# Second cross-attention of a two-layer decoder: the side work of each slot in another order

## The reference, cut to what matters

```
q, k, v = per head: x_h @ Wq.T, c_h @ Wk.T, c_h @ Wv.T
energy  = einsum('nqhd,nkhd->nhqk', q, k)
att     = softmax(energy / 16)
out     = einsum('nhql,nlhd->nqhd', att, v) @ Wo.T + bo
x       = layernorm(x + out)
```

## Time and profile before

| what | value |
|---|---|
| median of 3 runs | 2770.71 us (2766.24 to 2780.35) |
| the profiled execution | 2786.15 us |
| its span, first to last instruction | 2784.3 us |
| mean granted TensorE clock | 0.939 |
| PE busy | 2576.5 us (93%) |
| DVE busy | 1465.8 us (53%) |
| ACT busy | 1129.4 us (41%) |
| POOL busy | 1075.1 us (39%) |
| maxima of this stage on DVE (L1253) | 512 of 683 ns, 323.9 us busy |
| exponentials of this stage on ACT (L1203) | 256 of 1025 ns, 257.3 us busy |

### The profile page before, as it was taken

The page is one execution under the profiler, slowest core; times in us unless marked ns, Lnnn a source line. Parts: engine busy times, 40 slices in busy tenths (PEclk is TensorE's granted clock), DMA queues, the critical chain, the costliest instruction groups (busy, mean ns, idle before and its releaser), DMA issues.

```text
span 2784.3 us, 36664 instructions
## 1 busy us (share of the span) xinstructions
PE 2576.5 (93%) x13730; PEld 1534.9 (55%) x13734; DVE 1465.8 (53%) x3205; ACT 1129.4 (41%) x1614; POOL 1075.1 (39%) x727
## 2 busy tenths in 40 slices
PE   5786999999999999998799999958899999989997
PEld 3343555556556655664466666636344343468886
DVE  3444555555555555553533333347678777454545
ACT  3544344444444444443122222223377778731111
POOL 4666366765766666565000000052323333110001
PEclk8997899999999999999799999979699899889998
DMA  2001100000000000000899999720001000000000
GB/s 105 9 9 34 37 12 12 27 25 13 27 12 20 18 12 12 20 7 16 316 385 385 385 385 388 299 59 4 26 19 29 18 19 13 14 20 23 19 22 33
DMA packets 61345, 228.94 MB, mean 82 GB/s; under 512 B 17624, under 2 KB 31600, under 8 KB 45296
## 3 DMA queue, kind: packets, MB, share of 16 engines
q1 hardware_dynamic: 55280, 209.28, 20.5%
q0 software_dynamic: 3584, 9.84, 1.2%
q10 hardware_dynamic: 2304, 7.49, 0.7%
HBM read 214.37 MB, written 9.70 MB: 80 GB/s over the span
## 4 chain that ended last, share of the span: by engine, by line
PE 81%; DVE 7%; issue 4%; ACT 3%; POOL 3%; DMA 3%; SPq 0%; POOLq 0%; ACTq 0%; DVEq 0%
PE PS L686 8%; PE PS L1499 7%; PE PS L2098 7%; PE PS L669 6%; PE PS L717 5%; PE PS L1116 5%; PE PS L1131 5%; PE PS L1517 4%; PE PS L727 4%; PE PS L2086 4%; PE PS L701 3%; PE PS L1149 3%; PE PS L750 2%; DMA m_fb<-in_m_fb 2%; PE PS L673 2%
## 5 line engine op out<-in xcount | busy, mean ns | idle before, releaser
L950 POOL TENSOR_TENSOR x_A<-x_A,x_P 128x1024 f32<-128x1024 f32 x190 | 451.2, 2375 | 205.8 <-ACT x_P L797 191.8
L877 DVE CUSTOM_DVE_ANT_0 x_junk<-PS,x_mb 128x512 bf16<-128x512 f32 x512 | 330.9, 684 | 354.7 <-PE PS L701 354.4
L1253 DVE TENSOR_REDUCE y_Mx<-PS 128x1 f32<-128x512 f32 x512 | 323.9, 683 | 103.1 <-PE PS L1149 101.3
L797 ACT ACTIVATE x_P<-PS,x_kb 128x1024 f32<-128x1024 f32 x256 | 271.9, 1112 | 226.6 <-PE PS L673 224.6
L1203 ACT ACTIVATE y_P<-PS 128x1024 f32<-128x1024 f32 x256 | 257.3, 1025 | 99.4 <-PE PS L1131 96.8
L1499 PE MATMUL PS<-m_w,m_xt 128*128 128x512 f32 x624 | 282.9, 597 | 0.6 <-issue 0.6
L686 PE MATMUL PS<-x_P,x_V 128*64 128x512 f32 x1024 | 246.4, 602 | 0.0
L669 PE MATMUL PS<-x_Q,x_K 64*128 64x512 f32 x1536 | 231.6, 405 | 0.0
L2098 PE MATMUL PS<-n_xp,n_wp 128*128 128x512 f32 x816 | 212.0, 409 | 4.3 <-POOL n_wp L2214 4.3
L1149 PE MATMUL PS<-y_K,y_Q 16*128 16x512 f32 x512 | 192.1, 530 | 2.9 <-ACT y_F L1213 1.4
L1131 PE MATMUL PS<-y_Q,y_K 32*128 32x512 f32 (+1 forms) x1024 | 193.1, 461 | 0.3 <-ACT y_P L1203 0.2
(11 more groups left out here) (332 smaller groups left out, 4219.5 us busy)
## 6 DMA issues: line engine op xcount, KB each, us to landing
m_w<-in_m_w SPq DMA_DIRECT2D x39, 2048.0 KB, 11.3
m_fb<-in_m_fb SPq DMA_DIRECT2D x39, 1024.0 KB, 13.3
m_v<-in_m_w SPq DMA_DIRECT2D x39, 1024.0 KB, 7.1
x_w<-in_x_w SPq DMA_DIRECT2D x32, 384.0 KB, 3.1
ys<-m_yb SPq DMA_DIRECT2D x39, 128.0 KB
n_wg<-in_n_w SPq DMA_DIRECT2D x17, 256.0 KB, 2.8
x_cT<-in_ctxT SPq DMA_DIRECT2D x4, 1024.0 KB, 6.1
y_c<-in_ctxT SPq DMA_DIRECT2D x6, 512.0 KB, 3.7
```

The lines of the kernel that those rows point to most:

```text
L797: act.e.activation(Pt[gt % 6][:], PS[:, 2 * i:2 * i + 2, :], ACT.Exp, bias=kb[u // 8 % 2][:, kt:kt + 1], scale=scale).then_inc(s["exp"], 1)
L877: dve.e.tensor_tensor_reduce(junk[j % 2][:], ring.bank("max", v, j), mb[b % 2][:, half * 512:half * 512 + 512], 1.0, -3e38, ALU.add, ALU.m ...
L950: pool.e.tensor_tensor(A[u % 2][:], Pt[(gt - 1) % 6][:] if kt == 1 else A[u % 2][:], Pt[gt % 6][:], ALU.add).then_inc(s["add"], 1)
L1253: dve.e.tensor_reduce(Mx[v % 2][:, h, qt, half:half + 1], ring.bank("max", v, j), AX.X, ALU.max).then_inc(s["red"], 1)
```

## The change

Only the two tables of `l1_cross` change. In `beside`, k 1 goes from slot 1 to slot 2, q from 2 to 4, v 0 and 1 (with even units only) from 3 and 4 to 1 and 3, wo and res 0 to 3 from 3, 4, 5, 6 to 1, 3, 5, 7, and turn from 5 to 6. The transposes tp 0 and 1 leave `behind` of slots 4 and 6 for `beside` of slots 5 and 7. In `behind`, st 0 to 3 go from slots 4, 5, 6, 7 to slots 2, 4, 6 and slot 0 of the unit after, and nr 0 to 3 from slots 1 to 4 to slots 2 to 5. mq stays in slot 5, rec in 3, mul in 5, ev in 0.

```diff
-            beside = {0: [("k", 2, 0)], 1: [("k", 2, 1)], 2: [("q", 2, 0)], 3: [("v", 2, 0), ("wo", -2, 0), ("res", -2, 0)],
-                      4: [("v", 2, 1), ("wo", -2, 1), ("res", -2, 1)], 5: [("turn", 1, 0), ("wo", -2, 2), ("res", -2, 2)],
-                      6: [("wo", -2, 3), ("res", -2, 3)], 7: []}
-            behind = {0: [("ev", -1, 0), ("xb", 0, 0)], 1: [("nr", -3, 0)], 2: [("nr", -3, 1)], 3: [("rec", -1, 0), ("nr", -3, 2)],
-                      4: [("st", -2, 0), ("nr", -3, 3), ("tp", -3, 0)], 5: [("mul", -1, 0), ("st", -2, 1)],
-                      6: [("st", -2, 2), ("tp", -3, 1)], 7: [("st", -2, 3)]}
+            beside = {0: [("k", 2, 0)], 1: [("v", 2, 0), ("wo", -2, 0), ("res", -2, 0)], 2: [("k", 2, 1)],
+                      3: [("v", 2, 1), ("wo", -2, 1), ("res", -2, 1)], 4: [("q", 2, 0)], 5: [("tp", -3, 0), ("wo", -2, 2), ("res", -2, 2)],
+                      6: [("turn", 1, 0)], 7: [("tp", -3, 1), ("wo", -2, 3), ("res", -2, 3)]}
+            behind = {0: [("ev", -1, 0), ("xb", 0, 0), ("st", -3, 3)], 1: [], 2: [("st", -2, 0), ("nr", -3, 0)], 3: [("rec", -1, 0), ("nr", -3, 1)],
+                      4: [("st", -2, 1), ("nr", -3, 2)], 5: [("mul", -1, 0), ("nr", -3, 3)], 6: [("st", -2, 2)], 7: []}
```

## The result

The changed kernel takes 2790.49 us, the kernel before 2778.05 in the same comparison (medians of 20 runs each): ratio **1.0039**, 95% interval 1.0024 to 1.0055, some 11 us slower. The forecast was +7 us (1.0025), the range 2761 to 2794. Of the 12.5 us between the 2778 us forecast and the 2790.49 measured, 7.3 are the kernel before itself, whose median rose from 2770.71 (3 runs) to 2778.05 (20 runs). The profiled executions are no guide to the total: that of the changed kernel has a span of 2782.6 us, shorter than the 2784.3 of before, since outside this stage, where both run the same code, it happened to be 5.2 us shorter (2297.1 against 2302.3). So I read the stage in parts.

A forecast was written before the change was run, and what follows sets the result against it. PE and DVE were taken to starve each other in turn. Reordered slots -0.4, hand-overs +4.0, lead-in and end +3.4 made +7.0 us, added to the median 2770.7 for 2778 us; range 2761 to 2794.

The forecast's parts named there:

- Prices of slots: Units' slots, start to start: full after full 3.58 us, full after bare 4.1, bare after full 1.95.
- odd unit: Odd unit without batch work: full and bare slots alternate, 24.2 us against 24.80, a gain of 0.6.
- Even unit: Even unit without batch work: bare slots only 5 and 7, 26.4 us against 26.65, a gain of 0.3.
- Pair with batch work: Two units with batch work: all 16 slots full, 57.8 us plus 0.3 for statistics, against 56.43; 1.7 lost.
- Unit behind it: Unit after the two with batch work: starts after a full slot and so gains 0.5 us more.
- Rival A: Units: a single bare slot leaves no debt, odd units 22.0 us, even 25.8; some -14 us, 2757; chance 0.13.
- rival B: Hand-overs: rows late and dearer, net 1.4 us at each of twelve, 3 from the rest, 2791 us; chance 0.22.
- Hand-over: Passage between units: rows land 6.5 to 7.3 us into slot 6; PE stalls 0.5 to 1.3, net 0.5, eight times, +4.0.
- The body: Units after the lead-in: reordered slots -0.4 us, stalls at eight hand-overs +4.0, late rows into unit 15 +1.3.
- Lead-in: Before unit 0: q last in unit -2 costs +0.9 us, fewer maxima behind the turn in unit -1 +1.2.
- the late turn: Turn in slot 6, rows late: +4.0 us over eight hand-overs, +1.2 in the lead-in, +1.3 into unit 15.
- Waits: Before units' first scores: PE waits for a DMA or nothing visible, 0.5 to 1.3 us, about ten times; DVE's wait near 100.

The follow-up runs named there:

- e3: The changed kernel with the four DMAs that put the negated maxima into the queries' rows made one; ratio to the kernel before 0.9970.
- e7: The kernel before with the fourth maximum ahead of the values in every slot, bare ones too; ratio to the kernel before 1.0046.
- e1: The changed kernel with the turn back in slot 5, all else in its new slots; ratio to the kernel before 0.9971.
- e5: The changed kernel with the turn yet one slot later, in slot 7; ratio to the kernel before 1.0486.
- e2_turn_late: The kernel before with the turn alone moved to slot 6; ratio to the kernel before 1.0091.
- e4: The kernel before with the four row DMAs made one; ratio to the kernel before 1.0015.
- e6: The changed kernel with one row DMA, fourth output projection in slot 6, transposes behind slots 5 and 7, old lead-in order; ratio to the kernel before 0.9962.

## Why the prediction came out right, and where not

The direction, the mechanism (rows that come late) and the range held. By its steps:

- *Prices of slots.* Full behind a single bare 4.1: 3.99 and 4.09. Bare behind full 1.95: 1.97, or 2.17 where a key or query projection stands ahead that itself follows a bare slot; there PE waits 0.20 us for the exponential that ACT ran after the projection's two copies. Then in e3, where rows are in time: odd unit 24.2: 24.44. Even unit 26.4: 26.35. Pair with batch work 58.1: 57.8. Unit behind it 23.7: 23.87. e7 confirms the reason, the fourth maximum's place. Rival A falls with it. (Its even unit of 25.8 was a slip: six slots of 3.58 and two of 1.92 make 25.3. So was the edge of rival B: 13.9 less 3.0, over twelve hand-overs, is 0.9 and not 1.1.)
- *Hand-over.* From copy to landing 4.0 to 4.56: 4.22 to 4.33 where PE stood for the rows, but 4.58 and 4.80 into units 9 and 4, where the four issues took 2.7 and 2.9. Turn 1.3 to 1.5 into slot 6: 1.28 to 1.39. Stall 0.5 to 1.3: mostly 1.0 (slot 7 2.89), with 3.57 and not 4.0 in slot 0, so net 0.5 as taken. Unit 8 was to have room from the slow clock; that spell was elsewhere, and PE stood there too (slot 7 of unit 7 2.88). The body was forecast at -0.4 + 4.0 + 1.3 = +4.9 (one hand-over of it in unit 0); units 1 to 14 at the full clock are +4.2. The Trainium skill's rule to issue a DMA early and wait late (DMA: Bandwidth & Descriptors, "Rules for kernel authors") spoke against this change, and the runs agree: with the rows in time, as in e1 or e3, the same reordering gains 0.3%. The Trainium skill's fixed cost of about 2.0 us, from which the prediction drew its estimate of 0.3 us more for each hand-over (DMA: Bandwidth & Descriptors, "Anatomy of one DMA"), stands in that section for DMAs issued by GpSimd. These are issued by SP, and the scores ran 1.2 us behind the end of the last issue (2049.12 to 2050.29), some 1.7 behind its start; the measurement decides.
- *Lead-in.* +2.1 forecast, +3.5 measured. e1 has the turn early and +1.2, so the projections' places cost that (0.9 forecast) and the turn 2.3 (1.2 forecast).
- *The step that was mis-sized* is the late turn: 4.0 in the body, 1.2 in the lead-in and 1.3 at the end. Taking the lateness away, by e1 or by e3, gives 19 us and not 6.5; putting it into the kernel before costs 25. By slots alone the 6.5 is good: e3 takes 5.0 + 1.7 = 6.7 away. What was missing is the clock, which I had left alone. Behind the longest of the stalls PE runs its next slots at the lower level: unit 4 took 32.6 us in both profiles of the changed kernel and not 26.87.
- *Why the sum still fits.* The kernel before has a slow spell of its own in units 1 to 14, in both profiles. Compared pair by pair, the two profiles of each give +3.5 and +6.3 for the stage, less than the measured 11 (6.7 to 15.3). But both profiled executions of the kernel before, 2786 and 2793 us, are long ones for it (medians 2778.05 and 2771.9), so the profiles show it with more of the lower clock than it mostly has; e7 says the same. A way round this is to compare at equal clock. Time at the lower level is 2 x (1 - mean clock) x span. Straight lines through the timed executions, read off at 300 us of it, give an estimated span of 2775 to 2778 us for the kernel before (56 executions in three comparisons) and 2784 for the changed one (20). So +6 to +9 at equal clock, where the slots make it 3.5 + 4.2 = 7.7 and the forecast was 7.0. For e7 the same reading gives +12, by slots 11.9. What lies above 7.7 in the measured 11 would then be the clock, and that it is as little as 3 us is luck: nothing in the prediction says that its effects in the two kernels would nearly cancel.
- *Waits.* I expected "for a DMA or for nothing visible", 0.5 to 1.3 us, ahead of about ten units: it is ten, units 0 to 5, 8, 9, 13 and 15, the DMA named ahead of unit 0 alone, with PE idle for 1.64 us there and for 0.47 to 1.05 ahead of the others. DVE's wait for the maxima, forecast near 100, is 94.2.

## What to carry to other kernels

Before a step that issues DMAs is moved later, follow its chain to whoever waits (here turn, copy, five issues of 0.6 us, landing: 5.5 us) and lay it against the slots that are left. Where such a chain is tight, shorten it instead: one DMA for four rows made the reordering a gain, and brought nothing where there was slack. Price a slot from start to start by what stands before it, and count kinds of slots; that gave every kind of unit to within 2%, while shares of busy time said only that PE is full. And where the granted clock moves from execution to execution, ask for each difference what it is at equal clock: a profile shows one execution, and here both profiles of the kernel before were of long ones.

## What the runs showed of the hardware

A stall of TensorE can cost more than its length. With some 2.8 us of idleness ahead of every unit (e5) the granted clock of units 1 to 14 fell to 0.74 of full speed on average, and the same matmuls were busy for 94 us more. The rest of this is on units 1 to 14. Behind stalls of 1.0 us (slot 7 of 2.9 to 3.0 us) no spell followed. Behind the longer ones of e2_turn_late (slot 7 of 3.2 to 4.1 us, PE idle for 0.8 to 1.7) one followed each time, in both profiles. Of the two longer ones of the changed kernel one did it and one did not (3.4 yes, 3.3 no), so the length alone doesn't sort them. Spells also start in a turn slot behind a bare slot, with no long stall at all (in the kernel before, the changed one, e3, e4 and e6). In e1 no turn stands behind a bare slot, and its two profiles have no spell; in e7 turns do, and its one profile has none either. That is what was seen together; what in those slots lets the clock fall was not taken apart.
